# Attention decay exponents: key side summed on TensorE, one exponential per head pair

## The reference, cut to what matters

```
log_f = log_sigmoid(fg);  cs = cumsum(log_f)
log_D[s, t] = cs[s] - cs[t] + ig[t]          (t <= s, else -inf)
D = exp(log_D - max over t)
C = (q k^T / sqrt(dh)) * D
h = C / (max(|sum C|, exp(-max)) + eps) @ v,  then a norm over each head
```

## Time and profile before

| what | us |
|---|---|
| median of 3 runs (lowest to highest) | 3332.16 (3329.63 to 3335.16) |
| the profiled execution, its own time | 3335.54 |
| its span, first to last instruction | 3333.8 |
| PE busy in the span | 3059.0 (92%) |
| DVE, ACT, POOL busy in the span | 1941.6, 1277.3, 1039.7 |
| TensorE clock granted, mean over the span | 0.973 of full |

### The profile page before, as it was taken

How to read it: one execution, slowest core, us unless ns; L and a number is a source line. 1 busy time by engine, 2 the same in 40 slices (tenths; PEclk the granted TensorE clock), 3 DMA queues, 4 the chain that set the end, 5 groups by cost and what they waited for, 6 DMA issues and landing times.

```text
span 3333.8 us, 60389 instructions
## 1 busy us (share of the span) xinstructions
PE 3059.0 (92%) x23964; PEld 2407.0 (72%) x24092; DVE 1941.6 (58%) x5529; ACT 1277.3 (38%) x2860; POOL 1039.7 (31%) x949
## 2 busy tenths in 40 slices
PE   4888898888988828999999999999999999999998
PEld 3677777776777616777777777778778778778886
DVE  4788887888888765544545544544553554553332
ACT  3678877788887731111112112113112112211210
POOL 3456656566565631111211111121111112112111
PEclk9899999999999958999999999999999999999999
DMA  3143333433334241213213222223123223212211
GB/s 106 53 140 116 129 116 115 141 116 124 121 119 138 78 122 42 46 28 79 42 36 102 34 46 73 34 47 100 32 34 71 48 35 91 57 31 41 68 31 25
DMA packets 140065, 250.67 MB, mean 75 GB/s; under 512 B 31456, under 2 KB 31456, under 8 KB 139784
## 3 DMA queue, kind: packets, MB, share of 16 engines
q1 hardware_dynamic: 106104, 170.80, 15.3%
q0 software_dynamic: 28672, 67.65, 11.5%
q10 hardware_dynamic: 5008, 8.36, 0.8%
HBM read 137.23 MB, written 101.19 MB: 72 GB/s over the span
## 4 chain that ended last, share of the span: by engine, by line
PE 55%; DVE 5%; DMA 2%; issue 1%; ACT 0%; POOL 0%; DVEq 0%; ACTq 0%; POOLq 0%
PE UP L1434 27%; PE DN L1460 26%; PE TT L1413 2%; DMA w_raw<-in_L_ffn_W_down 1%; DVE c_early L1243 1%; DVE c_within L1185 1%; DVE c_hit L1174 0%; DVE c_cand L1205 0%; PE c_bank L1160 0%; DVE c_begun L1184 0%; ACT z L1386 0%; DVE xT_lo L1471 0%; DVE down_lo L1072 0%; DVE mid_lo L1491 0%; DVE y L1511 0%
## 5 line engine op out<-in xcount | busy, mean ns | idle before, releaser
L1360 POOL DMA_INDIRECT out_x<-y,slots x128 | 201.2, 1572 | 1687.3 <-DVE y L1513 1687.3
L1460 PE MATMUL DN<-down_hi,mid_hi 128*128 128x512 f32 x1408 | 588.5, 418 | 0.0
L1386 ACT ACTIVATE z<-UP,bup 128x512 f32<-128x512 f32 (+1 forms) x352 | 240.9, 686 | 881.6 <-PE UP L1434 858.2
L1434 PE MATMUL UP<-xT_hi,up_hi 128*128 128x512 f32 (+1 forms) x1408 | 554.6, 394 | 2.8 <-DVE xT_lo L1471 1.5
L1434 PE MATMUL UP<-xT_hi,up_lo 128*128 128x512 f32 (+1 forms) x1408 | 555.9, 395 | 0.0
L1434 PE MATMUL UP<-xT_lo,up_hi 128*128 128x512 f32 (+1 forms) x1408 | 552.5, 392 | 0.0
L1460 PE MATMUL DN<-down_hi,mid_lo 128*128 128x512 f32 x1280 | 505.5, 395 | 0.0
L1460 PE MATMUL DN<-down_lo,mid_hi 128*128 128x512 f32 x1280 | 504.8, 394 | 0.0
L1489 DVE CAST mid_hi<-z 128x512 fp32r<-128x512 f32 (+1 forms) x352 | 151.1, 429 | 498.2 <-ACT z L1386 486.9
L1369 ACT ACTIVATE xT_hi<-TT 128x512 fp32r<-128x512 f32 x128 | 76.3, 596 | 731.6 <-PE TT L1413 731.6
L1434 PEld LDWEIGHTS UP<-xT_hi,up_hi 128*128 128x128 f32 (+1 forms) x1408 | 260.4, 185 | 71.5 <-ACT z L1386 6.4
(11 more groups left out here) (229 smaller groups left out, 5115.8 us busy)
## 6 DMA issues: line engine op xcount, KB each, us to landing
xs<-in_x SPq DMA_DIRECT2D x32, 1024.0 KB, 8.1
kraw<-in_ctx SPq DMA_DIRECT2D x32, 1024.0 KB, 6.7
out_x<-xs SPq DMA_DIRECT2D x32, 1024.0 KB, 5.4
rows_scratch<-xfb SPq DMA_DIRECT2D x32, 1024.0 KB, 4.3
w_raw<-in_L_ffn_W_down SPq DMA_DIRECT2D x40, 512.0 KB, 4.6
w_raw<-in_L_ffn_W_up SPq DMA_DIRECT2D x16, 682.5 KB, 4.1
mid_hi<-mid_hi ACTq DMA_DIRECT2D x32, 86.0 KB
mid_lo<-mid_hi ACTq DMA_DIRECT2D x32, 84.0 KB
```

The costliest lines, as they stand in the source:

```text
L1360: pool.indirect_dma_start(out_rows, bass.IndirectOffsetOnAxis(ap=slots[:, m:m + 1], axis=0), y[:, t, :], None, compute_op=ALU.add).then_in ...
L1386: act.activation(z[0:r, k % 2, :], UP[k % 3][0:r, :], ACT.Silu, bias=bup[0:r, e // 2, f:f + 1]).then_inc(s["z"], 1)
L1434: mm = pe.matmul(UP[k % 3][0:r, :], weights.up[wa][:, c, f * P:f * P + r], xT[xa][:, c, :], start=first, stop=(c == CH - 1 and wa == 1))
L1460: mm = pe.matmul(DN[m % 2][:, :], lhs, rhs, start=first, stop=(f == FCH - 1 and lhs is parts[-1][0]))
```

## The change

- The key side of the exponent is summed by PE too. POOL gets a new step `split_climb(b)`, placed between its work for b3 and `weigh_v(b1)`: from `rise` it makes `climb`, in two instructions of 128 x 128 (high parts in rows 0 to 7 of a chunk, low parts in rows 8 to 15), in two buffers, and counts `rp` up. PE multiplies `climb` with a pattern of ones (`pick`).
- `EX` is laid out by chunk pair (a = 0 for chunks 0 and 1, a = 1 for chunks 2 and 3), with both heads side by side. A chunk pair has its gate rows in one half of the partitions, so all products use half the rows: for each pair of heads four mask products of 64 x 64 weights over 512 columns (a second mask `maskswap` has the key halves exchanged), two of `climb` (64 x 128 over 512), four of `sel` with `peaks` (64 x 128 over 256).
- In `decays(b1, 0)` PE waits for `rp` behind the mask products and before those of `climb`, then for the peaks.
- ACT takes one exponential of 128 x 1024 for a pair, without a bias; its wait for the turned gates goes. `dd` counts once for a pair.
- `turn_gates` turns two tiles instead of three; `tm` shrinks by a third. DVE waits for `rp` of the sequence before, ahead of L914. `constants` on POOL gets a second mask and `pick`.

```diff
+        maskneg = sb("maskneg", [P, SEQ], BF16); maskswap = sb("maskswap", [P, SEQ], BF16)
+        climb = sb("climb", [P, 2, P], FP32R); climb_low = sb("climb_low", [P, P], FP32R)
+        pick = sb("pick", [P, PAIRS, 2, 2], FP32R)
...
+                    step(pool.tensor_tensor(wt[:, 0:2], own[:, 0:2], own[:, 2:4], ALU.add))
+                    step(pool.tensor_tensor(pick[:, :, :, :].rearrange("k p a j -> k (p a) j"), draft[:, :, 0:2],
+                                            spread(wt[:, 0:2], 1, HEADS), ALU.mult))
...
+                    step(pool.memset(maskswap[:, :], 0.0))
+                    for half, first in ((slice(0, DH), -DH), (slice(DH, P), 0)):
+                        m = maskswap[half, :].rearrange("p (j s) -> p j s", j=TILES)
+                        step(pool.affine_select(out=m, in_=m, compare_op=ALU.is_ge, fill=-BIG, base=first,
+                                                pattern=[[0, TILES], [1, P]], channel_multiplier=-1))
...
+                def split_climb(b):
+
+                    wait_taken(pool, "shift", b, 0)
+                    if b >= 2:
+                        pool.wait_ge(s["ee"], 2 * PAIRS * (b - 1))
+                    step(pool.tensor_scalar(climb_low[:, :], rise[:, :], lows[:, 0:1], None, ALU.mult))
+                    pool.tensor_tensor(climb[:, b % 2, :], rise[:, :], climb_low[:, :].bitcast(FP32), ALU.subtract).then_inc(s["rp"], 1)
+                    pool.wait_ge(s["rp"], b + 1)
...
                     if live(b1):
+                        split_climb(b1)
                         weigh_v(b1)
...
-                    if p == 0:
-                        wait_taken(act, "turn", b, 0)
                     if g >= CRING:
                         act.wait_ge(s["af"], g - CRING + 1)
-                    for par in range(2):
-                        h = 2 * p + par
-                        act.wait_ge(s["ee"], 2 * g + par + 1)
-                        for j in range(TILES):
-                            ins = act.activation(C[:, 2 * (g % CRING) + par, j * P:(j + 1) * P], EX[:, par, j * P:(j + 1) * P], ACT.Exp,
-                                                 bias=tm[:, b % 2, 1, j, h:h + 1])
-                        ins.then_inc(s["dd"], 1)
+                    act.wait_ge(s["ee"], 2 * g + 2)
+                    first = 2 * (g % CRING)
+                    act.activation(C[:, first:first + 2, :].rearrange("t r (a n) -> t r a n", a=2),
+                                   EX[:, :, :].rearrange("t a (r n) -> t r a n", r=2), ACT.Exp).then_inc(s["dd"], 1)
...
-                    pe.transpose(t[:, P:2 * P], rise[:, :], ident[:, :])
-                    pe.transpose(t[:, 2 * P:3 * P], nr[:, :], ident[:, :])
+                    pe.transpose(t[:, P:2 * P], nr[:, :], ident[:, :])
...
                     if g:
-                        pe.wait_ge(s["dd"], 2 * g)
+                        pe.wait_ge(s["dd"], g)
+                    top, end = slice(0, DH), slice(DH, P)
+                    for a, r, mask in ((0, top, (maskneg, maskswap)), (1, end, (maskswap, maskneg))):
+                        for t, m in zip((top, end), mask):
+                            pe.matmul(EX[t, a, :], identb[r, r], m[r, :], start=True, stop=False, skip_group_check=True)
+                    if p == 0:
+                        pe.wait_ge(s["rp"], b + 1)
+                    for a, r in ((0, top), (1, end)):
+                        ones_of = pick[r, p, :, :].rearrange("k a j -> k (a j)")
+                        pe.matmul(EX[:, a, :], climb[r, b % 2, :], spread(ones_of, 2, P), start=False, stop=False, skip_group_check=True)
                     if p == 0:
                         pe.wait_ge(s["xm"], b + 1)
                     for par in range(2):
-                        pe.matmul(EX[:, par, :], identb[:, :], maskneg[:, :], start=True, stop=False)
-                    for par in range(2):
-                        pe.matmul(EX[:, par, :], sel[:, 2 * p + par, :], peaks[:, b % 2, :], start=False, stop=True).then_inc(s["ee"], 1)
+                        for a, r in ((0, top), (1, end)):
+                            half = slice(a * 2 * P, (a + 1) * 2 * P)
+                            mm = pe.matmul(EX[:, a, par * 2 * P:(par + 1) * 2 * P], sel[r, 2 * p + par, :], peaks[r, b % 2, half],
+                                           start=False, stop=True, skip_group_check=True)
+                            if par:
+                                mm.then_inc(s["ee"], 1)
...
                     dve.wait_ge(s["qk"], g + 1)
+                    dve.wait_ge(s["dd"], g + 1)
                     for par in range(2):
-                        dve.wait_ge(s["dd"], 2 * g + par + 1)
...
+                    if b >= 1:
+                        dve.wait_ge(s["rp"], b)
                     dve.tensor_tensor(rise[:, :], g[:, 0:P], cs[:, :], ALU.subtract).then_inc(s["td"], 1)
```

More of the change, by code:

```diff
@@ L125, in attention @@
         later = sb("later", [P, P]); own = sb("own", [P, TILES]); unseen = sb("unseen", [P, TILES]); spot = sb("spot", [P, 2, HEADS]); lows = sb("lows", [P, TILES])
-        gb = sb("gb", [P, 2, PAIRS]); tm = sb("tm", [P, 2, 3, TILES, HEADS])
-        maskneg = sb("maskneg", [P, SEQ], BF16)
+        gb = sb("gb", [P, 2, PAIRS]); tm = sb("tm", [P, 2, 2, TILES, HEADS])
+        maskneg = sb("maskneg", [P, SEQ], BF16); maskswap = sb("maskswap", [P, SEQ], BF16)
+        climb = sb("climb", [P, 2, P], FP32R); climb_low = sb("climb_low", [P, P], FP32R)
+        pick = sb("pick", [P, PAIRS, 2, 2], FP32R)
         gW = sb("gW", [P, 2 * CH, QD])
@@ L147, in attention @@
                  "ee dd qk cc af an sq sr x2 x2v lex smx hs vc uv "
-                 "dchain achain pchain prep1 prep2 prep3").split()
+                 "rp dchain achain pchain prep1 prep2 prep3").split()
         s = {n: sem("a_" + n) for n in names}
@@ L831, in head_variances @@
                     n = nsb[:, b % 2, :, :, :].rearrange("p j h w -> p (j h) w")[:, :, DH:DH + 1]
-                    low_bound = tm[:, b % 2, 2, :, :].rearrange("p j h -> p (j h)").unsqueeze(2)
+                    low_bound = tm[:, b % 2, 1, :, :].rearrange("p j h -> p (j h)").unsqueeze(2)
                     t = top[:, :].unsqueeze(2)
@@ L862, in turned_gates @@
                     t = filled(dve, "turn", b, 0)
-                    t4 = t[:, 0:3 * P].rearrange("p (k j h) -> p k j h", k=3, h=QD)
+                    t4 = t[:, 0:2 * P].rearrange("p (k j h) -> p k j h", k=2, h=QD)
                     for par in range(2):
```

## The result

The changed kernel takes **3473.8 us** (median of 4 runs, 3471.92 to 3474.98), the kernel before 3333.0 beside it (4 runs, 3329.63 to 3335.16). The ratio is 1.0423, with a 95% interval of 1.0405 to 1.0441: **141 us slower**. The profiled execution took 3471.9, with a span of 3470.2.

The account below looks back on a forecast made before the run. A loop of waits set by the DVE branch bounds the kernel, no engine filling it. Period 34.18 + 3.1 (delay) + 2.3 (clock) = 39.6 against 34.50, 5.1 x 30 = 153 us more: 3485 us, range 3410 to 3545.

Parts of the forecast that it names:

- The new wait: PE in pair 0 waits for POOL's `split_climb` behind L221; period grows by 3.1 us (2.7 to 5.3).
- The clock: PE's 5.5 us idle stretch drops it to half clock through `turn_gates`: 2.3 us for each iteration.
- my lower end of 1.96: Low bound of the half-clock cost: 1.96 us, from an earlier iteration with 6.3 us at half clock.
- My 2.8: High bound of the half-clock cost: work from PE's release to the end of `turn_gates`, 2.8 us, doubles.
- Pairs 1 to 3: PE's smaller products there change by -0.2 to +1.4 us a pair, up to 4.2 an iteration; costed at nothing.
- the cover: PE's idle five us before pair 0; peaks may come 4.3 us later before slower PE products matter.
- The side-by-side price of a pair: PE's ten new products of a pair take 0.64 us side by side, 1.7 one after another.
- The rule on tile shapes: Tiling mode changes drain TensorE; the change behind `sel` would add 0.11 to 0.27 x 30 = 3 to 8 us.
- ACT: One exponential a pair takes 1.0 us instead of 2.16, some 4.6 less an iteration, worth nothing by itself.
- Rival 1: Clock holds despite PE's wait, leaving the delay alone: 2.8 x 30 = 83 us, 3415 us; chance 0.13.
- Rival 2: Half clock lasts far past the gates, about 5 us lost: 7.8 x 30 = 233, 3565 us; chance 0.10.
- Rival 3: `rp` isn't late and lighter ACT releases the turn's 0.75 wait: at most 22 us faster, 3310; chance 0.03.

Follow-up runs that it names:

- the run with the repeats: Changed kernel with pair 0's four mask products repeated 20 times while PE would wait for `climb`: 3408.34 us (one run).
- the run with more masks: Changed kernel with the mask products of pairs 1 to 3 made six times instead of once: 3458.56 us (one run).
- a shorter loop alone: Kernel before, with ACT's `turned_rows(b4, 1)` moved ahead of the work that waits for the peaks: 3321.14 us, ratio 0.9952.
- the shorter loop with the change: Changed kernel with `split_climb` early, plus ACT's `turned_rows(b4, 1)` ahead of the work that waits for the peaks: 3318.68 us, ratio 0.9941.

## Why the prediction was right

The forecast was 3485 and the measurement is 3473.8, 11 us lower and inside the range; the sign and the mechanism held. By its steps:

- **The new wait.** PE's wait is ended by `split_climb` and is 5.1 long, as said. POOL's two instructions took 0.60 and 0.45 (0.55 and 0.41 were worked out), `climb` came 1.23 behind L223 instead of 1.12, and PE took it up 0.05 later, not 0.37. `climb` and `sel` then took 0.65 at full clock (906.76 - 906.11 in the run with the repeats), not 0.43. These three errors cancel, which is luck: the delay is 3.06, predicted 3.1. That it is this wait, the kernel before with the wait alone shows, and that it is POOL's place, the kernel with `split_climb` early.
- **The clock.** 2.3 was the term that was too large: it measured 2.01, near my lower end of 1.96. How much of `turn_gates` lies at half clock changes from iteration to iteration: its last product takes 0.29 at 957.47, as at full clock, and 0.44 at 918.23, in the iteration before, which took 39.42. My 2.8 had all of it at half clock. The row of the wait has a clock of 0.75 and the next one 0.50, so the clock had also fallen in the middle of the wait already, where it costs nothing. What is left over, 4.75 x 30 = 143 against 5.1 x 30 = 153, is 10 of the 11 us.
- **Pairs 1 to 3.** Costed at nothing because of the cover, and the cover is shown twice: three us more PE work cost nothing with the wait, and without the wait the peaks came 0.58 later. The side-by-side price of a pair, 0.64, was too low: 927.78 - 926.79 = 0.99 in the trace. Masks, `climb` and `sel` take 0.34, 0.32 and 0.33, where I had 0.21 or 0.22 for each. That excess isn't simply a price for each change of shape: from `climb` to `sel` the shape stays 64*128, and the step is 0.32 all the same.
- **The rule on tile shapes.** One change can be read by itself: in the run with more masks the step from the last repeat to `climb` is 918.05 - 917.74 = 0.31, against 0.21 from repeat to repeat. So 0.10 more goes where the shape changes, and the type and the size of the weights with it; no run parts these. The Trainium skill's page "TensorEngine Tiling (Array Packing)", section "Tiling Modes", says that a change of mode drains TensorE. The step agrees with a price, a little under the 0.11 to 0.27 that I had drawn up, but doesn't prove it.
- **ACT.** 1.01 for the exponential, predicted 1.0; 133.6 us less busy, predicted some 140. In the changed kernel it hides behind the wait, as predicted; with the wait gone, eight exponentials without a bias take as long as one.
- **The rivals.** Rival 1, the clock holds, gives the delay alone: forced by filler products, that took 3408, where I had worked out 3415. It isn't what happens by itself. Rival 2, half clock far past the gates, didn't come: the stretch from 958 on is at 1.00. Rival 3 said 22 us of gain if `climb` were in time; moved up, it is in time, and the gain is 3331.1 - 3324.2 = 7. Its step, that a lighter ACT releases the turn, held for 0.49 of the 0.75 and no further, since ACT's copy then waits for the peaks; and the dearer pairs 1 to 3, which it didn't count, took that back.

What stays open: why the clock holds in every steady iteration once the masks stand ahead of the wait, when a shorter loop alone lets it fall in ten of 26. In the shorter loop with the change, whose masks stand ahead as well, it falls in two of 26. Moving them takes some 0.5 us out of the wait (1.17 in an iteration that fell, 0.7 here) and puts work right ahead of it, and no run parts the two. Each period comes from one profiled execution, so a difference of a few hundredths between two kernels is not a finding.

## What to carry to other kernels

A helper of two small instructions costs what it makes the next engine wait, not what it takes: 1.2 us of POOL work cost 4.75 us an iteration behind twelve long instructions and nothing behind four. Before moving work to an engine that seems free, write down when the input is needed and when that engine's queue gets to it. Count an idle stretch of TensorE twice, for the delay and for the clock behind it (here two fifths of the loss), and put work that needs no input ahead of the wait.

## What the runs showed of the hardware that I had not expected

- More PE work made a kernel faster: 3 us an iteration ahead of the wait took it from 3473.8 to 3458.6 (one run). The work fitted into the wait, which fell from 5.1 to 1.9, and the clock rose from 0.91 to 0.95.
- Four half-row mask products side by side take 0.21 us when the same shape follows, and 0.31 to 0.34 when products of another shape, type and weight size do. The rows of the weight loads (PEld) in the changed kernel show one difference: the loads for `climb` start only with its products, while those for `sel`, in the same shape, start 0.21 ahead of theirs (927.45 - 927.24). No run tests how much of the price that is.

```profile
927.13 0.19 PEld L672 LDWEIGHTS EX<-pick,climb 64*128 64x128 f32 x2 [0.23 <-issue]
927.24 0.41 PEld L678 LDWEIGHTS EX<-peaks,sel 64*128 64x128 f32 x4
```

- An exponential of 128 x 128 took 0.18 of ACT's time where it has no bias from a tile (136.3 / 752) and 0.27 where it has one (200.5 / 744). The Trainium skill's page "ScalarE: Activation LUTs", section "What ACT_TABLE_LOAD costs", puts a pointer operand at about 93 ns, and these rows agree (0.09 by busy time; by the mean of one instruction, 380 - 303 ns, it is 0.08).
